# A fused attention and expert layer on one core: context scores wait tile by tile, and GpSimd makes the low part of another tile

## What is computed

```python
x = x + xattn(layernorm(x), ctx)   # softmax((q k^T) / sqrt(512)) v, q from x, k and v from ctx
x = x + attn(layernorm(x))         # 16 heads, causal, low-rank projections
x = x + ffn(layernorm(x))          # shared experts, and 16 routed experts, 4 per token
```

## Time and profile before

| | us |
|---|---|
| median of 3 runs (lowest, highest) | 362.99 (362.04, 364.71) |
| the profiled execution | 367.77 |
| its span, from the first to the last instruction | 366.0 |
| mean granted TensorE clock over the span | 0.967 of full |
| TensorE matmul busy | 342.7 (94%) |
| VectorE busy | 241.0 (66%) |
| ScalarE busy | 189.1 (52%) |
| GpSimd busy | 94.9 (26%) |

### The profile page before, as it was taken

The page is one execution under the profiler, slowest core; times in us unless marked ns, Lnnn a source line. Parts: engine busy times, 40 slices in busy tenths (PEclk is TensorE's granted clock), DMA queues, the critical chain, the costliest instruction groups (busy, mean ns, idle before and its releaser), DMA issues.

```text
span 366.0 us, 6994 instructions
## 1 busy us (share of the span) xinstructions
PE 342.7 (94%) x2530; PEld 239.9 (66%) x2530; DVE 241.0 (66%) x475; ACT 189.1 (52%) x428; POOL 94.9 (26%) x114
## 2 busy tenths in 40 slices
PE   6999799999999989998879889999998999999996
PEld 4887567677677757766669779887643444444344
DVE  2875978746588377576782468880534677778587
ACT  2547574635566574484754452502134677777520
POOL 3600500000012011443472140004336554432000
PEclk9999999999999999996977998989999999999999
DMA  6982689976222345071050460699834453331573
GB/s 234 402 360 99 236 339 422 375 244 223 86 88 87 107 166 218 29 277 69 3 193 10 144 258 1 243 376 411 318 108 154 148 175 120 126 107 57 202 288 115
DMA packets 17185, 69.70 MB, mean 190 GB/s; under 512 B 2816, under 2 KB 3328, under 8 KB 14592
## 3 DMA queue, kind: packets, MB, share of 16 engines
q1 hardware_dynamic: 12768, 56.93, 41.4%
q0 software_dynamic: 3520, 11.54, 9.2%
q10 hardware_dynamic: 864, 0.79, 0.7%
HBM read 61.91 MB, written 7.34 MB: 189 GB/s over the span
## 4 chain that ended last, share of the span: by engine, by line
PE 74%; DVE 12%; ACT 6%; issue 3%; DMA 2%; another core or an unknown queue 1%; POOL 1%; ACTq 0%; DVEq 0%
PE bank L1582 9%; PE bank L2030 9%; PE bank L2062 9%; PE bank L1584 9%; PE bank L1583 9%; PE bank L1892 8%; PE bank L1999 2%; DMA raw<-in_wkT 2%; PE bank L2073 2%; PE bank L2041 2%; PE bank L1732 2%; DVE cT L1283 2%; PE bank L1785 2%; PE bank L1742 1%; PE bank L1837 1%
## 5 line engine op out<-in xcount | busy, mean ns | idle before, releaser
L1892 PE MATMUL bank<-ring,wT 128*128 128x384 f32 x128 | 44.0, 487 | 0.7 <-ACT wT L894 0.7
L2030 PE MATMUL bank<-WX,xsT 128*32 128x256 f32 (+1 forms) x256 | 38.0, 380 | 0.9 <-DVE xsT L1492 0.9
L2062 PE MATMUL bank<-WX,hsT 128*32 128x512 f32 (+1 forms) x128 | 38.2, 598 | 0.0
L1283 DVE TENSOR_TENSOR cT<-ring_T,cT 128x512 fp32r<-128x512 f32 x45 | 31.0, 732 | 6.6 <-ACT cT L752 6.6
L1892 PEld LDWEIGHTS bank<-ring,wT 128*128 128x128 f32 x128 | 23.6, 190 | 14.2 <-ACT wT L894 0.9
L2030 PEld LDWEIGHTS bank<-WX,xsT 128*32 128x32 f32 x256 | 17.8, 110 | 22.0 <-issue 11.9
L1514 DVE COPY down_copy<-WX 128x1024 f32 x32 | 21.0, 696 | 15.0 <-PE bank L2062 14.8
L2030 PE MATMUL bank<-up_copy,xsT 128*32 128x256 f32 x384 | 30.7, 379 | 0.0
L2062 PE MATMUL bank<-down_copy,hsT 128*32 128x512 f32 x192 | 30.7, 598 | 0.0
L752 ACT CAST cT<-ring_T 128x512 fp32r<-128x512 f32 x48 | 27.0, 618 | 6.5 <-PE bank L1584 6.3
L688 POOL DMA_INDIRECT xs<-x_rows,from_row x20 | 19.6, 982 | 40.7 <-DVE to_row L1237 27.3
(11 more groups left out here) (296 smaller groups left out, 901.3 us busy)
## 6 DMA issues: line engine op xcount, KB each, us to landing
WX<-in_experts SPq DMA_DIRECT2D x16, 1024.0 KB, 6.0
ring_T<-in_ctxT SPq DMA_DIRECT2D x16, 768.0 KB, 7.1
ring<-in_ctx SPq DMA_DIRECT2D x16, 768.0 KB, 5.2
WX<-y_rows SPq DMA_DIRECT2D x4, 1024.0 KB, 8.2
raw<-in_experts SPq DMA_DIRECT2D x3, 1024.0 KB, 5.0
raw<-in_wqT SPq DMA_DIRECT2D x4, 256.0 KB, 5.7
res<-in_x SPq DMA_DIRECT2D x4, 256.0 KB, 8.2
raw<-in_woT SPq DMA_DIRECT2D x1, 1024.0 KB, 4.8
```

Source lines behind the costliest of these rows:

```text
L1283: V_.tensor_tensor(cT[:, g % 2, 1, t, :], ring_T[:, g % RING_T, t, :], f32(cT[:, g % 2, 0, t, :]), ALU.subtract).then_inc(cTlo_ok, 1)
L1892: last = mm(bank[B_O][:, 0:TD], wT[:, g % 2, k * P:(k + 1) * P], ring[:, g % RING, k, :], start=(c == 0 and k == 0), stop=(c == NCH - 1 an ...
L2030: last = mm(bank[B_H[g % 2]][q * SLOT:(q + 1) * SLOT, 0:IC * P], xsT[:, g % 2, c * P + q * SLOT:c * P + (q + 1) * SLOT], w, start=c == 0, ...
L2062: last = mm(bank[B_Y[g % 2]][q * SLOT:(q + 1) * SLOT, :], hsT[:, g % 2, m * P + q * SLOT:m * P + (q + 1) * SLOT], w, start=m == 0, stop=m ...
```

## The change

In `chunk_scores` the wait for all low parts of the chunk goes from the head of the function to each of its three tiles. For chunks 2, 3 and 4, GpSimd makes the low part of tile 0 as soon as its high part is there, where it made that of tile 2 after all three high parts; VectorE makes tiles 1 and 2 of these chunks in place of 0 and 1. The number of low parts, who makes how many, and every count are as before.

```diff
@@ GpSimd
             for g in POOL_LO:
-                pool.wait_ge(cThi_ok, TC * (g + 1))
-                nc.gpsimd.tensor_tensor(cT[:, g % 2, 1, TC - 1, :], ring_T[:, g % RING_T, TC - 1, :], f32(cT[:, g % 2, 0, TC - 1, :]),
+                pool.wait_ge(cThi_ok, TC * g + 1)
+                nc.gpsimd.tensor_tensor(cT[:, g % 2, 1, 0, :], ring_T[:, g % RING_T, 0, :], f32(cT[:, g % 2, 0, 0, :]),
                                         ALU.subtract).then_inc(cTlo_pool, 1)
@@ VectorE
                 if 1 < step < G:
-                    chunk_lo(step, 0)
+                    if step not in POOL_LO:
+                        chunk_lo(step, 0)
                     chunk_lo(step, 1)
-                    if step < U_STEP and step not in POOL_LO:
+                    if step < U_STEP:
                         chunk_lo(step, 2)
@@ TensorE, chunk_scores
-                    pe.wait_ge(cTlo_ok, low_parts(g))
-                    if pool_parts(g):
-                        pe.wait_ge(cTlo_pool, pool_parts(g))
                     if g == 0:
                         pe.wait_ge(qklo_ok, TC)
@@
                     for t in range(TC):
+                        if g in POOL_LO and t == 0:
+                            pe.wait_ge(cTlo_pool, pool_parts(g))
+                        else:
+                            pe.wait_ge(cTlo_ok, low_parts(g) - TC + t + 1)
                         last = split_mm(bank[s_bank(g)][:], (qk_h[:, t, tok(b)], qk_l[:, t, tok(b)]),
                                         (cT[:, g % 2, 0, t, :], cT[:, g % 2, 1, t, :]), t == 0, t == TC - 1)
                     last.then_inc(s_mm, 1)
```

## The result

| | median of 12 runs (lowest, highest), us | profiled span, us |
|---|---|---|
| before | 364.69 (362.04, 365.87) | 366.0 |
| after | 362.23 (361.56, 364.66) | 361.0 |

The ratio after to before, estimated over all runs, is 0.9949, with a 95% interval of 0.9925 to 0.9972: 1.85 us less (1.0 to 2.7). The two medians of the table are 2.46 us apart, which is inside that interval. The kernel before has a median of 364.69 us over 12 runs, where the three runs known at first gave 362.99. So the forecast of a gain, 1.6 us, is to be held against the ratio. The forecast of a time, 361.4 us, started from three runs of which two happened to be short, and 362.23 was measured.

The account below looks back on a forecast made before the run. The prediction took TensorE to bound the kernel, in flight 342.7 of 366.0 us. Gaps of 2.90 us removed less 1.29 returning gave 1.6: 363.0 - 1.6 = 361.4 us, range 359.8 to 364.2.

Parts of the forecast that it names:

- The place and the ceiling: TensorE at 34.0 to 48.5 us: its 3.06 us idle cap the gain; the steady part has nothing to shorten.
- The layout, chunk by chunk: Chunks 2 to 4: TensorE starts at 37.83, 40.15 and 42.5 us; gaps of 1.24, 0.77 and 0.89 us shrink.
- The sum: Product line 1892 starts at 46.90 us, not 48.53: 2.90 us of gaps removed, 1.29 come back, 1.6 gained.
- the standstill between GpSimd and VectorE: Low parts in chunks 2 to 4: whoever comes second waits; VectorE's ends 0.55 us after GpSimd's, which costs 1.15 to 1.29.
- what is late next: After chunk 4: TensorE waits for batch 0's exponential from 44.68 to 45.55 us, a new gap of 0.87 us.
- (b): Chunks 3 and 4: VectorE's chain costs 0.5 us more each, gain shrinks to 0.6, time 362.4 us; chance 0.17.
- (c): Waits inside chunks break TensorE's stream: 32 x 0.11 = 3.5 us, so slower, 364.9 us; chance 0.08.
- (d): Softmax of batch 0 comes sooner than laid out: gain 2.1 to 3.1 us, time 360.4 us; chance 0.07.
- (e): Gain made at 48 us is lost later through TensorE's granted clock: about 363.0 us; chance 0.10.

Follow-up runs that it names:

- e4: Kernel before, with VectorE making all low parts of chunks 2 to 4 and GpSimd none: distance 11.10 us, ratio 0.9982 to before.
- e1: Kernel before, with TensorE waiting tile by tile and GpSimd still making the last tile's low part: distance 12.23 us, ratio 1.0007 to before.
- e6: Changed kernel with a wait on each of a chunk's 9 score matmuls, in place of each third: distance 10.80 us, ratio 0.9960 to before.
- e3: Changed kernel, with VectorE making all low parts of chunks 2 to 4 and GpSimd none: distance 10.81 us, ratio 0.9929 to before.
- e7: Changed kernel, with GpSimd making only chunk 4's last low part, after VectorE's tile before it: distance 10.49 us, ratio 0.9942 to before.

## Why the prediction was right

**The place and the ceiling.** The window of the earlier trace rows named one stretch with 3.06 us idle and a steady part with none. Busy time by window of the kernel after:

```profile
34.00:48.50 14.50, 12.96 (x58) 9.31 (x57) 10.40 (x21) 10.90 (x20) 4.15 (x3) 1.00 0.65 253
51.50:56.60 5.10, 5.10 (x23) 3.60 (x22) 4.98 (x11) 2.95 (x7) 0.00 (x0) 1.00 0.92 350
```

TensorE is busy for 12.96 us of the first stretch instead of 11.44, so 1.54 us are still idle, and 1.52 of 3.06 were taken; the steady part is as full as it was.

**The layout, chunk by chunk.** With 0.27 us added for this execution's later start, the forecast against the trace:

| | forecast + 0.27 | after |
|---|---|---|
| GpSimd's three starts | 35.81, 39.05, 41.12 | 35.81, 39.05, 41.09 |
| chunk 2 starts | 38.10 | 38.10 |
| chunk 3 starts | 40.42 | 40.50 |
| chunk 4 starts | 42.77 | 42.80 |
| scores of chunk 3 moved | 43.77 | 43.73 |
| transposes | 45.82 | 45.76 |
| product | 47.17 | 47.09 |

The largest miss is 0.08 us. For GpSimd's third part the table takes the moment when its high part is ready; the prediction let it stand until 41.2 and end at 42.4, which is 42.67 with the 0.27, and the trace's row holds the standing and ends at 41.09 + 1.56 = 42.65. In chunk 2 the prediction also had VectorE stand behind GpSimd for 0.13 us; the trace shows its two low parts in 1.29 us, as without GpSimd, and nothing hung on it. The sum was 1.6 and the trace has 1.7. The term that carried it is the standstill between GpSimd and VectorE, read from two ends 0.55 us behind GpSimd's, and "what is late next", VectorE's way to the maximum of batch 0: without the 0.87 us that come back ahead of the transposes the forecast would have been 1.6 + 0.87 = 2.5 us or so.

**What the prediction didn't separate.** It laid out the two edits together. The runs part them: 0.28 us for the waits, 1.41 for GpSimd's earlier start, and that second gain is not one of help but of less harm, since GpSimd's absence gives the same 1.41 (e4). The expectations of e1 to e4, worked out with the same rules, named the distance from chunk 1's last start, which is 1.58 us less than the one in the table (10.80 against 9.22 for the kernel after): 10.8, 9.5, 9.2 and 9.6 us were expected, and 10.65, 9.52, 9.23 and 9.52 measured.

**The rivals.** (b), a VectorE chain that eats a full us, fell with the line at 47.09. (c), a price for waits inside the stream, fell with e6. (d) didn't come: the ceiling isn't reached because of the exponential. (e), a shift that is lost or changed later, is half true. The shift itself isn't lost. At the end of the first block the product's last start is 156.6 us before and 155.1 after, 1.5 us less, or 1.8 with the 0.27 by which this execution came later. To the end of the program it can be followed in e1, which gains 0.28 us, and e6, which gains as much as the change, 1.43 us more. Their mean granted clock is the same, 0.976, and so it is by window: 0.91 from 160 to 180 us, 0.74 from 180 to 200, 0.94 from 200 to 230, full elsewhere. Their spans are 361.1 and 360.9 us. From VectorE's first move (36.05 and 37.34) to the end it is 325.1 us in e1 and 323.6 in e6, 1.5 us less, so all of it arrives. The two spans differ by 0.2 us only because e6 came to this place 1.3 us later.

What varies is the rest of an execution. The profiled spans before and after differ by 5.0 us, far more than the runs' 1.85. One piece of it is the granted clock; windows of TensorE alone (length, busy, clock, DMA share, GB/s), before and then after:

```profile
243.00:246.00 3.00, 3.00 (x24) 0.86 1.03 396
246.00:249.00 3.00, 3.00 (x10) 0.57 1.00 418
```

```profile
243.00:246.00 3.00, 3.00 (x17) 1.00 1.01 421
246.00:249.00 3.00, 3.00 (x14) 1.00 1.01 426
```

Part of these windows ran at the lower of the clock's two levels, 1.2 in place of 2.4 GHz, in one execution and not in the other, with TensorE busy for the full 3 us of every window in both. (1 - 0.86) x 3 + (1 - 0.57) x 3 = 1.7 us of TensorE's time went there. With the shift that makes 3.4 us, and ScalarE's first `hsT` (line 993, in the last block) does start 3.4 us later before than after, 263.88 against 260.47. The other 1.6 us come between 264 and 296 us, in the experts. In that stretch stands a pause of VectorE, one row in the waits of the kernel before that none of the nine later traces has:

```profile
DVE up_copy L1507 <- remote: 3.2, 1, 3.2
```

What it waited for the profile doesn't name, and how much of the 1.6 us it cost is open too: 1.0 of them are there before it, at ScalarE's third `hsT` (272.17 against 267.71). The traces of e1 and e4, of which one has the GpSimd part and one the waits of the kernel before, don't have the pause either, so nothing ties it to the change. A reader who had compared the two spans would have taken 5.0 us for what is 1.7.

**What was luck.** The place, the layout and the sum are borne out by the traces. That the runs' 1.85 us lies so near is in part chance: the groups of runs described in the last section are some 2 us apart, and the gain comes out as 0.6 or 2.3 us, depending on which groups are compared.

## What to carry to other kernels

Before handing VectorE's work to GpSimd, look for the two side by side in the trace: here a 0.68 us subtraction became a 1.29 us one that shut VectorE out, and the helper was worth nothing at the head of the chunk (e3 against the change) and minus 1.4 us at its end (e4 against before). One part beside a move from a bank was worth 0.3 us (e7). When several engines feed one, lay out the new order instruction by instruction up to the next thing that is late, and take the gain at that point and not at the gap that closes. Put the shared work beside instructions that read a bank, not beside those that read two tiles of SBUF.

## What the runs showed of the hardware

A wait on a matmul whose count has been reached cost nothing measurable: 96 more of them left starts 0.23 us apart (e6). After a real stop the first matmul of 512 columns held the next one off for 0.30 to 0.34 us instead of 0.23.

GpSimd's subtraction of 128 x 512 took 1.28 or 1.29 us whenever nothing held it, and a VectorE one that waited for it ended 0.54 to 0.56 us after it, not 0.68.

Single runs of one kernel lie in groups by their mean granted clock. Of the kernel before on both chips, 21 runs at 0.976 have a mean of 362.8 us and 32 at 0.967 one of 365.0; of the kernel after, 20 runs of 24 are at 0.972 with a mean of 362.2, and the 12 runs before at that same clock have one of 364.5. So from the shortest group to the shortest it is 0.6 us less, and at the same clock 2.3. The groups are further apart than the change is worth, so three runs can't show it. Whether a shift of 1.7 us changes how often a kernel falls into which group is open: no run was made for it alone.
